# Four GNN layers on one core: neighbours' rows moved by one scatter instead of gathered in the clipped attention

## The reference

```python
# layer 0: eight heads, gated by the edge's attributes
e = leaky(src_part[row] + dst_part[col] + edge_attr @ eb_w.T + eb_b)
attn = exp(e - max_of_dst) / sum_of_dst
out = segment_sum(h[row] * sigmoid(edge_attr @ eg_w.T + eg_b) * attn, col)
# layer 1 (here "dst" is edges[:, 0], which is the graph's src; "src" is edges[:, 1], the graph's dst)
h = node_states @ kernel
scores = exp(clip(leaky(score_dst[dst] + score_src[src]), -2, 2))
out = segment_sum(h[src] * (scores / scores_sum[dst]), dst)
# layer 2: edge_attr summed by row, and an MLP
edge_aggr = zeros.at[row].add(edge_features)
# layer 3: four heads, softmax over the 8 highest scores of each row
```

## Time and profile before

| | |
|---|---|
| median of 3 executions | 11,575.82 us (11,573.05 to 11,590.34) |
| the profiled execution | 11,594.04 us, of which the span 11,592.2 |
| mean granted clock of TensorE | 0.703 of full |
| busy: PE, DVE, ACT, GpSimd | 7351.4, 6759.5, 1898.0, 7519.6 us |
| TensorE's full clock, its other level | 2.4 GHz, 1.2 GHz |

### The profile page before, as it was taken

The page is one execution under the profiler, slowest core; times in us unless marked ns, Lnnn a source line. Parts: engine busy times, 40 slices in busy tenths (PEclk is TensorE's granted clock), DMA queues, the critical chain, the costliest instruction groups (busy, mean ns, idle before and its releaser), DMA issues. The chain is left out here.

```text
span 11592.2 us, 207186 instructions
## 1 busy us (share of the span) xinstructions
PE 7351.4 (63%) x46899; PEld 6169.2 (53%) x46900; DVE 6759.5 (58%) x14152; ACT 1898.0 (16%) x5455; POOL 7519.6 (65%) x7664
## 2 busy tenths in 40 slices
PE   3488888889999027760068888888657870076443
PEld 2266666668999016650046666666436760066333
DVE  8977777774333068860334444444557889977336
ACT  0033333332222021100021111111110000011000
POOL 0077777777777717777147777777506779977772
PEclk9967766675555558885568888888758985578556
DMA  1055555552222217762544444444206981188564
GB/s 47 16 154 153 154 153 153 153 153 88 86 86 86 90 39 210 213 190 90 29 78 105 106 106 106 105 106 107 70 4 184 257 220 38 39 223 223 157 158 115
DMA packets 2024581, 1406.19 MB, mean 121 GB/s; under 512 B 393331, under 2 KB 1861108, under 8 KB 2024340
## 3 DMA queue, kind: packets, MB, share of 16 engines
q1 hardware_dynamic: 989254, 579.30, 17.2%
q0 software_dynamic: 218976, 470.22, 16.7%
q10 hardware_dynamic: 816272, 355.84, 12.7%
HBM read 1058.59 MB, written 347.72 MB: 121 GB/s over the span
## 5 line engine op out<-in xcount | busy, mean ns | idle before, releaser
L1349 POOL DMA_INDIRECT ca_xg<-table,ca_idx x1856 | 1818.3, 980 | 909.5 <-issue 505.6
L1523 POOL DMA_INDIRECT z_xg<-table,srci x1664 | 2072.0, 1245 | 507.1 <-issue 507.1
L620 POOL DMA_INDIRECT gr_xg<-table,gr_idx x1612 | 1621.6, 1006 | 866.6 <-ACT gr_idx L694 447.3
L909 POOL DMA_INDIRECT sorted<-sc_er,sc_idx x1612 | 1674.6, 1039 | 709.0 <-issue 394.5
L1455 PE MATMUL ca_ps<-ca_row,ca_oh 128*128 128x257 f32 x3712 | 1222.8, 487 | 7.1 <-DVE ca_row L1413 7.1
L1583 PE MATMUL z_ps<-z_wrow,z_oh 128*128 128x132 f32 x3712 | 750.5, 371 | 596.2 <-issue 219.0
L1583 PEld LDWEIGHTS z_ps<-z_wrow,z_oh 128*128 128x128 f32 x3712 | 664.7, 269 | 682.0 <-issue 668.8
L1455 PEld LDWEIGHTS ca_ps<-ca_row,ca_oh 128*128 128x128 f32 x3712 | 843.9, 238 | 150.9 <-DVE ca_row L1413 7.9
L432 PEld LDWEIGHTS xe_px<-scores,xe_oht 128*128 128x128 f32 x3608 | 824.9, 333 | 0.3 <-issue 0.3
L641 PE MATMUL gr_psg<-gr_wg,gr_eT 128*128 128x136 f32 x3224 | 821.2, 395 | 0.0
L432 PE MATMUL xe_px<-scores,xe_oht 128*128 x3608 | 773.3, 344 | 0.0
(11 more groups left out here) (377 smaller groups left out, 14539.6 us busy)
## 6 DMA issues: line engine op xcount, KB each, us to landing
ca_row<-sorted SPq DMA_DIRECT2D x464, 256.0 KB
z_buf<-gathered ACTq DMA_DIRECT2D x464, 256.0 KB, 3.7
ag_buf<-gated ACTq DMA_DIRECT2D x451, 256.0 KB
gathered<-z_xg SPq DMA_DIRECT2D x416, 256.0 KB
gated<-gr_y SPq DMA_DIRECT2D x403, 256.0 KB
gr_eT<-in_attr_t SPq DMA_DIRECT2D x402, 256.0 KB
sc_er<-in_attr SPq DMA_DIRECT2D x402, 256.0 KB
z_lob<-target_row ACTq DMA_DIRECT2D x416, 128.0 KB
```

Of the source, the lines that this page charges most:

```text
L620: nc.gpsimd.indirect_dma_start(out=xg[:, u, j, :], out_offset=None, in_=v.table[:, :], in_offset=bass.IndirectOffsetOnAxis(ap=idx[:, u, j: ...
L909: nc.gpsimd.indirect_dma_start(out=self.rows_out[:, :], out_offset=bass.IndirectOffsetOnAxis(ap=idx[:, u, j:j + 1], axis=0), in_=er[:, u, ...
L1349: nc.gpsimd.indirect_dma_start(out=xg[:, u, j, :], out_offset=None, in_=v.table[:, :], in_offset=bass.IndirectOffsetOnAxis(ap=idx[:, u, j: ...
L1523: nc.gpsimd.indirect_dma_start(out=xg[:, u, j, :], out_offset=None, in_=v.table[:, :], in_offset=bass.IndirectOffsetOnAxis(ap=v.dsti[:, t: ...
```

## The change

One scatter remains. It is made in layer 1, after the histogram has been counted in the gate stage, and it writes rows of RW = 260 numbers: the dst node's transformed features and score (129), the attributes (128), the taking node's score, and both keys. The clipped attention then needs only these rows.

- `stage_gate` has the gates, the counting of the histogram, and the expansion of dst scores: ACT's `spread` asks for the group's keys on all partitions, DVE's `hot` compares them with the block's node numbers (which gives the transposed one-hot at once), PE's `look` and DVE's `far` add the scores. Gathers take their indices from `srci`.
- `stage_aggregate` loads on SP and multiplies on GpSimd.
- `stage_node_rows` keeps the nodes' features and scores in SBUF (`held`) and scatters the self loops' second copies and the padding.
- `stage_move` finds the positions as the rank did, expands the held rows to the edges (`spread`, `hot`, `expand`, `fill`), and scatters 4 tiles a group from S = 8 slots. `steps` has two more rows: the slot (2), and the step after which a group is whole (3), for which SP's `ready` waits; `follows` says whether a step adds to the one before.
- `stage_neighbours` loads `sorted` (1040 B a row), makes the weights in five operations of 4 elements a partition on GpSimd and an exp on ACT, multiplies and sums. The meta loads are issued on ACT's queue at its start.

The functions `turned`, `high`, `middle`, `counts`, `same`, `below_middle` and the other parts of the rank are as before, but for `lookups` and `choose`, which handle 100 columns a tile (positions and scores) instead of 50. `counts` for g > 0 still waits for the copy of g − 1 (`s_ohtb`) and for `running`.

```diff
-RW = 132
+SCORE, TAKING = C + 1 + C, C + 2 + C
+RW = 260
+SLOTS = 8
...
+def stage_gate(nc, v, e_score, gated, hist, steps):
...
+                for g in range(GE):
+                    u = g % R
+                    if g >= R:
+                        pool.wait_ge(s_y, g - R + 1)
+                        pool.wait_ge(s_es, g - R + 1)
+                    for j in range(G):
+                        t = g * G + j
+                        nc.gpsimd.indirect_dma_start(
+                            out=xg[:, u, j, :], out_offset=None, in_=v.table[:, :],
+                            in_offset=bass.IndirectOffsetOnAxis(ap=v.srci[:, t:t + 1], axis=0)).then_inc(s_xg[u], 16)
+
...
+                def look(k, u, use):
+                    b = pe.value_load(steps[0:1, 1, ds(k, 1)], min_val=0, max_val=NBX - 1)
+                    if later(k, 2):
+                        pe.wait_ge(s_add, k - 1)
+                    pe.wait_ge(s_hot, k + 1)
+                    for j in range(G):
+                        last = nc.tensor.matmul(psx[u % 2][:, j * X8:(j + 1) * X8], hot_t[:, u, j * P:(j + 1) * P],
+                                                flat(v.scores[:, ds(b, 1), :]), start=True, stop=True)
+                    last.then_inc(s_got, 1)
+
+                pipeline(pe, GE, (gates, 0), (count, 1), (look, 1, KE), ring=R)
+                nc.tensor.matmul(psc[:, 0:NBX], v.zeros[:, :], v.zeros[:, 0:NBX], start=False,
...
+                def spread(k, u, use):
+                    g, _ = step_of(nc, act, steps, k, GE)
+                    if later(k, R):
+                        act.wait_ge(s_hot, k - R + 1)
+                    act.dma_start(keys[:, u, :], v.dst_row[:, ds(g * (G * P) + 1, G * P)].broadcast_to(
+                        [P, G * P])).then_inc(s_key[u], 16)
...
+                pipeline(act, GE, (spread, 0, KE), (sigmoid, 1), ring=R)
...
+                def hot(k, u, use):
+                    b = dve.value_load(steps[0:1, 1, ds(k, 1)], min_val=0, max_val=NBX - 1)
+                    if later(k, R):
+                        dve.wait_ge(s_got, k - R + 1)
+                    dve.wait_ge(s_key[u], use * 16 + 16)
+                    nc.vector.tensor_scalar(hot_t[:, u, :], keys[:, u, :], v.node[:, ds(b, 1)], None,
+                                            ALU.is_equal).then_inc(s_hot, 1)
...
+                pipeline(dve, GE, (onehots, 0), (hot, 0, KE), (gated_rows, 1), (scores, 2), (far, 3, KE), ring=R)
...
+def stage_aggregate(nc, v, name, rows, keys, steps, n_steps, groups, weights, heads, acc):
...
+            @block.gpsimd
+            def _(pool):
+                def weighted(k, u, use):
+                    g, _ = step_of(nc, pool, steps, k, groups)
+                    if later(k, R):
+                        pool.wait_ge(s_mm, k - R + 1)
+                    weigh(nc.gpsimd, pool, k, u, use, g)
+
+                pipeline(pool, n_steps, (weighted, 0), ring=R)
...
+def stage_node_rows(nc, v, name, rhs, held, scores):
...
+                for b in range(NB):
+                    nc.gpsimd.indirect_dma_start(
+                        out=v.sorted[:, :], out_offset=bass.IndirectOffsetOnAxis(ap=v.loop_at[:, b:b + 1], axis=0),
+                        in_=loops[:, b, :], in_offset=None).then_inc(s_loop, 16)
+                pool.wait_ge(s_loop, 16 * NB)
...
+def stage_move(nc, v, held, run, steps, follows):
...
+                        sp.dma_start(rows[:, u, :, WH:WH + C], attr[:, ds(g * G, G), :]).then_inc(s_ld[u], 16)
...
+                def ready(g, u, use):
+                    n = sp.value_load(steps[0:1, 3, ds(g, 1)], min_val=1, max_val=KE)
+                    sp.wait_ge(s_put, n)
+                    sp.wait_ge(s_add, n)
+                    sp.sem_inc(s_ready, 1)
+
+                pipeline(sp, GE, (load, 0), (ready, 4), ring=S)
...
+                for g in range(GE):
+                    u, use = g % S, g // S
+                    pool.wait_ge(s_place, g + 1)
+                    pool.wait_ge(s_ld[u], use * 16 + (32 if g == GE - 1 else 16))
+                    pool.wait_ge(s_ready, g + 1)
+                    for j in range(G):
+                        t = g * G + j
+                        nc.gpsimd.indirect_dma_start(
+                            out=v.sorted[:, :], out_offset=bass.IndirectOffsetOnAxis(ap=place[:, t:t + 1], axis=0),
+                            in_=rows[:, u, j, :], in_offset=None).then_inc(s_sc[u], 16)
...
+                def expand(k, u, use):
+                    b = pe.value_load(steps[0:1, 1, ds(k, 1)], min_val=0, max_val=NBX - 1)
+                    if later(k, 2):
+                        pe.wait_ge(s_add, k - 1)
+                    pe.wait_ge(s_hot, k + 1)
+                    for j in range(G):
+                        last = nc.tensor.matmul(psx[u % 2][:, j // 2, (j % 2) * WH:(j % 2 + 1) * WH],
+                                                hot_t[:, u, j * P:(j + 1) * P], flat(held[:, ds(b, 1), :]),
+                                                start=True, stop=True)
+                    last.then_inc(s_got, 1)
+
+                pipeline(pe, GE, (expand, 1, KE), (lookups, 3), (same, 1), (counts, 0), ring=R)
...
+                def spread(k, u, use):
+                    g, _ = step_of(nc, act, steps, k, GE)
+                    if later(k, U):
+                        act.wait_ge(s_hot, k - U + 1)
+                    else:
+                        act.wait_ge(s_split, 5)
+                    act.dma_start(keys[:, u, :], v.dst_row[:, ds(g * (G * P) + 1, G * P)].broadcast_to(
+                        [P, G * P])).then_inc(s_key[u], 16)
+
+                def turned(g, u, use):
+                    if later(g, R):
+                        act.wait_ge(s_look, g - R + 1)
+                        act.wait_ge(s_q, g - R + 1)
+                    act.wait_ge(s_cnt, g + 1)
+                    nc.scalar.activation(ohtb[:, u, :], pst[:, :], ACT.Copy).then_inc(s_ohtb, 1)
...
+                def index(g, u, use):
+                    act.wait_ge(s_pos, g + 1)
+                    nc.scalar.activation(place[:, ds(g * G, G)], facts[:, ds(g * G, G), 0], ACT.Copy).then_inc(s_place, 1)
+
+                def put(k, u, use):
+                    g = act.value_load(steps[0:1, 0, ds(k, 1)], min_val=0, max_val=GE - 1)
+                    slot = act.value_load(steps[0:1, 2, ds(k, 1)], min_val=0, max_val=S - 1)
+                    act.wait_ge(s_free, g + 1)
+                    act.wait_ge(s_pos, g + 1)
+                    if later(k, 1):
+                        act.wait_ge(s_put, k)
+                    nc.scalar.activation(rows[:, ds(slot, 1), :, WH + C:RW].rearrange("p s t c -> p (s t) c"),
+                                         facts[:, ds(g * G, G), 1:4], ACT.Copy).then_inc(s_put, 1)
+
+                pipeline(act, GE, (spread, 0, KE), (turned, 0), (high, 1), (middle, 2), (index, 5), (put, 6, KE), ring=R)
+
+            @block.vector
...
+                def fill(k, u, use):
+                    g = dve.value_load(steps[0:1, 0, ds(k, 1)], min_val=0, max_val=GE - 1)
+                    slot = dve.value_load(steps[0:1, 2, ds(k, 1)], min_val=0, max_val=S - 1)
+                    dve.wait_ge(s_got, k + 1)
+                    dve.wait_ge(s_free, g + 1)
+                    if later(k, 1):
+                        dve.wait_ge(s_add, k)
+                    here = rows[:, ds(slot, 1), :, 0:WH].rearrange("p s (b t) c -> p (s b) t c", b=2)
+                    nc.vector.scalar_tensor_tensor(
+                        here, here, follows[:, ds(k, 1)],
+                        psx[u % 2][:, :, 0:2 * WH].rearrange("p b (t c) -> p b t c", t=2), ALU.mult,
+                        ALU.add).then_inc(s_add, 1)
...
+                pipeline(dve, GE, (hot, 0, KE), (below_middle, 3), (choose, 4), (onehots, 0), (running, 1),
+                         (below_high, 2), (earlier, 2), (position, 4), (fill, 3, KE), ring=R)
...
+def stage_neighbours(nc, v, steps, acc, meta, s_meta):
...
+                    sp.dma_start(row[:, u, :, :], src[:, ds(g * G, G), :]).then_inc(s_at[u], 16)
...
+                def score(k, u, use):
                     if later(k, R):
-                        pool.wait_ge(s_w, k - R + 1)
-                    pool.wait_ge(s_idx, k + 1)
-                    for j in range(G):
-                        nc.gpsimd.indirect_dma_start(
-                            out=xg[:, u, j, :], out_offset=None, in_=v.table[:, :],
-                            in_offset=bass.IndirectOffsetOnAxis(ap=idx[:, u, j:j + 1], axis=0)
-                        ).wait_op(s_one, 1, "sem-ge").then_inc(s_xg[u], 16)
-
-                pipeline(pool, KS, (gather, 0), ring=R)
+                        pool.wait_ge(s_exp, k - R + 1)
+                    pool.wait_ge(s_at[u], use * 16 + 16)
+                    nc.gpsimd.tensor_tensor(t[:, u, 0, :], row[:, u, :, C], row[:, u, :, SCORE], ALU.add).then_inc(s_sum, 1)
+
+                def parts(k, u, use):
+                    pool.wait_ge(s_sum, k + 1)
```

(66 more changed lines are left out.)

978 lines of the change are left out of this document (423 added, 555 removed).

## The result

The changed kernel takes 14,751.7 us (median of 4, 14,748.6 to 14,760.7) against 11,578.8 us before: ratio 1.2735, 95% interval 1.2716 to 1.2754, slower. I had written 14,800 and a range of 13,200 to 15,800. The profiled execution's span is 14,748.2 us.

The account below looks back on a forecast made before the run. GpSimd's gathers bound the old gate and attention stages; in the new stage_move a serial circle would. −358 − 1413 + 20 − 319 − 1217 + 10 + 6505 on 11,594 gave 14,822, as a median 14,800 us, range 13,200 to 15,800.

Parts of the forecast that it names:

- Steps 1 to 4: stage_move: expand waits for fill, turned for counts, the keys' request stands behind turned, hot waits for keys; a serial circle.
- T: Time of one stage_move turn, the sum of the circle's terms: 15.5 us, bounds 10.7 and 18.1.
- PE, half clock for the most part: stage_move: PE's expand, lookups, same and counts, 5.0 us at half clock, 2.5 at full; 4.7 taken.
- keys' landing: stage_move: 512 keys to 128 partitions, 256 KB, between rows of 1.6 and 3.7 us; 2.9 taken.
- DVE: stage_move: DVE's turn from hot to fill, operations and fill's two register loads, together 5.2 us.
- Gate: Gate stage: GpSimd's gathers cover the added work at 5.08 us an iteration; 2145 us against 2125.
- Aggregation: Aggregation: with the multiply on GpSimd, 2.1 us a step between 1.4 and 3.0; 947 us against 1266.
- Neighbours with their meta loads: Neighbours stage: 2.55 us a step, bounds 2.0 and 3.5, 1183 us against 2400; meta loads' 115 us only move.
- The faster one: stage_move: circle not closed, T = 5.5 us at GpSimd's or DVE's throughput, about 10,770 us; chance 0.07.
- The shorter circle: stage_move: keys' transfer hidden, T = 12.6 us, about 13,630 us; with PE at full clock 12,750; chance 0.17.
- A circle in the gate stage: Gate stage: keys' request waits behind sigmoid, 6.5 us an iteration instead of 5.08, +572, about 15,370 us; chance 0.06.
- Dear GpSimd arithmetic: GpSimd slow: 3.0 us a step in the aggregation (+406), 3.5 in the neighbours (+441), about 15,640 us; chance 0.08.

Follow-up runs that it names:

- all three: Changed kernel with keys asked for ahead, ACT's lags of the kernel before, and fill first in DVE's order: 10,393.7 us against 11,580.2 for the kernel before.
- keys from rows: On top of all three, the 13 meta loads left out, ACT copying keys from loaded rows: 13,358.2 us in the slow session, 10,277.2 (ratio 0.888) later.

## Why the prediction was right

**The circle.** Steps 1 to 4 were right, link by link, and the runs show it rather than only agree with it. Cutting the keys' link gave 10.21 us a turn (10.3 expected), moving fill alone 11.80 (12.0), all three 5.17, while doubling the work of the engine that only waits changed nothing. Cutting ACT's lag as well as the keys' gave 7.65 (7.3), which shows that the lag was a link, but what was left was not the circle that I had named (choose behind lookups, not running behind counts). That the new stage was the whole loss is shown too: with the same instructions in another order the changed kernel beats the one before.

**The terms of T.** 16.03 measured over the stage, 15.5 written; the one turn that the table takes apart was 16.39.

| term | written | one turn |
|---|---|---|
| PE, half clock for the most part | 4.7 | 4.72 |
| ACT from counts to the request | 2.6 | 2.83 |
| keys' landing | 2.9 | 3.94 |
| DVE | 5.2 | 4.90 |

The landing is the one that was mis-sized, by 1.0 us: I had the row of the same 256 KB at 3.7 and let the small source talk me down. The profile after gives a median of 3.7 for these keys. Against it DVE was 0.3 cheaper: fill's two register loads show no gap at all in the timeline (position at 7024.56, fill at 7025.04), where I had put 0.7; from fill's start to expand it was 0.88, where I had 0.60 and 0.1 for handing over.

**The stages.** Gate: 2212 us, 2145 written. Its turn was GpSimd's, 5.20 us as (2278.4 − 181.4)/403, not a circle; the last 48 steps took 2.4 each instead of 1.8. But PE came close to bounding the stage, which the prediction doesn't see. I had counted some 2.4 us of PE a turn, 1.06 of them for the gates; it was busy 2109.0 of the 2212 us. The gates alone are eight matmuls a group and not the four of the earlier trace rows, 1027.5 us in all, and look's matmuls have only 8 columns and still took 362 ns each, about as long as their 128x128 fp32 weight loads (329 ns):

```profile
L479 PE MATMUL g_psx<-scores,g_hot 128*128 x3608 | 840.2, 362 | 92.4 <-DVE e_score L568 87.0
```

That the stage came out near 2145 rests on GpSimd covering it and on a granted clock of 1.00; no run shows it at the slow clock.

Aggregation: 778 instead of 947, 1.72 a step. The GpSimd multiply took 1.21 us in the mean and 1.06 in the median; the estimate by the Trainium skill (GPSIMD Engine Reference, 3.1) was 1.1, and these rows agree with it. The stage that followed from that page, 631 us, was too short by 147, mine was too long by 169: the step did not get down to PE's 1.4. stage_move: 6727 instead of 6505, 403 × 0.53 = 214 of it by T. Neighbours with their meta loads: 1103 us (135 before the first sum, 968 for the steps), where 1183 + 115 was written: a step of 2.08 instead of 2.55. DVE bounds it, as written, but the timeline has one gap for a register load in a step and not two:

```profile
11001.59 0.75 DVE L1421 SCALAR_TENSOR_TENSOR n_oh<-iota,blk,n_row 128x512 f32<-128x512 f32 x1 [0.41 <-issue]
...
11002.26 0.69 DVE L1428 TENSOR_TENSOR n_row<-n_row 128x512 f32<-128x512 f32 x1
...
11002.86 0.42 DVE L1440 TENSOR_TENSOR acc<-acc,n_ps 128x257 f32 x1
```

Measured less written, these are +67, −169, +222 and −195 us, together −75; the sum of 14,822 stands against 14,750 of the profiled execution. So the closeness of the total, 0.3%, is partly luck; three of the four errors are 1.1 to 1.5% of it. Granted clock: 0.57 over stage_move's turns, near the half clock that I took; the gate stage ran at 1.00, where I had counted with the slow one.

**The rivals.** The faster one needed T under 7.49; it was 16.03. The shorter circle was not there but could be made, and then it was shorter than its price: with the keys asked for ahead the turn was 10.21 us and not 12.6, since hot, index, put and the issue left the circle together with the landing. A circle in the gate stage: none. Dear GpSimd arithmetic: no, 1.7 and 2.1 us a step.

## What to carry to other kernels

When a stage gets a new producer and consumer, write down for each engine what its first instruction of a turn waits for, and what stands last in the turn of the engine that releases it; if the list comes back to where it began within one turn, the turn costs the sum of all its links and not the longest. A DMA's request placed behind an unrelated wait on the issuing engine adds its whole landing to that sum, however many buffers it has. And try the order before the design: 30% of this kernel's time lay in two lines, one of lags and one of places, and the idea behind the change, one scatter and no gathers, was worth 10% (10,393.7 against 11,580.2) once they were right.

## What the hardware showed

The same program differs by 28% between two sessions here: the kernel before took 11,580 and 14,862 us. The expectations put this down to the chip. That is not shown: the record has chip number 12 for the first four runs, and number 14 both for the slow session (14,862.3 us) and for the later one (11,576.7 us), and whether these two are one chip it doesn't say. So it is a difference between sessions, steady within each (14,852 to 14,879 us in seven executions). Two rows place a part of it, DVE's product of the gate stage, in the version with all three in the first session and in the one with keys from rows in the slow one, 403 turns each:

```profile
L541 DVE TENSOR_TENSOR g_y<-g_gate,g_xg x403: 673/693/767, 193.5 to 2288.6; 128x512 f32<-128x512 f32 x135
```

```profile
L541 DVE TENSOR_TENSOR g_y<-g_gate,g_xg x403: 671/691/751, 193.9 to 2807.1; 128x512 f32<-128x512 f32 x135
```

5.21 us a turn against 6.50, with the operation itself as fast. In stage_move the turn of the version with keys from rows was 7.12 us, (7053.2 − 4189.8)/402, in the slow session and 5.19, (5726.5 − 3641.2)/402, in the later one. The stages without indirect DMAs took the same time (aggregation 770 us, neighbours 973), and the turn of 16 us, which had room, did as well.

The last layer lost most: from its first matmul to the last update it took 4446 us (8835.5 to 13,281.4) instead of 2760 (7556.9 to 10,317.0). More than all of that lies in its first part, in which ACT asks for keys, PE and DVE use them, and GpSimd gathers beside them: 2898 us (8835.5 to 11,733.2) instead of 696 (7556.9 to 8253.1). The layer's sums were even shorter, 870 us (12,402.6 to 13,272.4) instead of 1383 (8924.9 to 10,307.9); in the faster run the gathers still go on beside them. Of that part's 6656 matmuls these two stretches have 208 and 2171 (the first number in brackets); the gathers ended at 11,188:

```profile
9600.00:10200.00 600.00, 36.77 (x208) 28.68 (x208) 19.69 (x39) 0.00 (x0) 461.89 (x430) 0.51 0.39 102
...
10800.00:11400.00 600.00, 208.36 (x2171) 191.03 (x2172) 195.27 (x409) 0.00 (x0) 299.64 (x279) 0.65 0.46 122
```

DVE's sum behind these matmuls waited 2250.7 us for a DMA. (The profile names `ag_buf<-gated`, a load of an earlier stage; by the program, what stands behind this wait is the landing of the keys; the profile doesn't show it.) GpSimd's own gathers were not slower over the stretch, 2307 us (8881.1 to 11,188.1) instead of 2600 (7604.1 to 10,203.9). So in this part the loads of the ordinary queue starved beside indirect DMAs and recovered when these were done. Why is open; nothing was run on it. For a comparison it means that totals must come from one session, with the kernel before run beside, and that a stage's own first and last start can be compared across sessions only where no indirect DMAs set its pace.

A DVE operation with two inputs in SBUF (the one-hot of the aggregation) took 1.04 us in the mean, and 1.55 in the turn shown above, beside GpSimd's multiply, and 0.75 without it. The Trainium skill (SBUF — State Buffer, Who interferes with whom) says that such an instruction contends with a GpSimd instruction that reads SBUF. These rows agree with it, and show that DVE pays here; what GpSimd's multiply pays no run shows, since none has it alone.
